# Moving the side jobs of two attention layers to other steps, with the first layer's layer norm on GpSimd

## What is computed

```python
x = _layernorm(x + _L0_attn_ref(x, ...))
x = _layernorm(x + _L0_ffn_ref(x, ...))
x = _layernorm(x + _L1_attn_ref(x, ...))
x = _layernorm(x + _L1_ffn_ref(x, ...))
...
attn = softmax(einsum('bhnd,bhmd->bhnm', q, k) * ATTN_SCALE)
out = einsum('bhnm,bhmd->bhnd', attn, v)
return out.reshape(B, N, C) @ w_proj + b_proj
```

## Time and profile before

| | us |
|---|---|
| median of 3 runs | 1456.69 |
| lowest, highest | 1455.31, 1460.36 |
| the profiled execution | 1455.56 |
| its span in the trace | 1453.8 |
| TensorE busy | 1117.4 (77% of the span) |
| VectorE busy | 1095.9 (75%) |
| ScalarE busy | 841.6 (58%) |
| GpSimd busy | 540.3 (37%) |

### The profile page before, as it was taken

One profiled execution on the slowest core, in us unless ns is written; L12 is line 12 of the kernel. 1 busy time (PEld: TensorE's weight loads), 2 busy tenths in 40 slices (PEclk: granted clock), 3 DMA queues, 4 the chain that ended last, 5 costly groups with the idle time before them and its releaser, 6 DMA issues. The chain is left out here.

```text
span 1453.8 us, 36143 instructions
## 1 busy us (share of the span) xinstructions
PE 1117.4 (77%) x11411; PEld 778.6 (54%) x11411; DVE 1095.9 (75%) x2949; ACT 841.6 (58%) x1840; POOL 540.3 (37%) x568
## 2 busy tenths in 40 slices
PE   2699999999999995139999999999999948103220
PEld 1466666666666653126777777777777724002120
DVE  4589999999999976526677676676776756898996
ACT  1277777777777763616666666666666635103554
POOL 5323233332332203154455444554444142003555
PEclk9899999999999998559999999999999978655555
DMA  1655556556465513044444444444444202000111
GB/s 45 151 124 134 137 120 140 126 128 140 116 138 133 116 29 122 11 120 103 115 114 113 108 115 105 116 115 104 119 103 115 67 16 101 0 0 0 30 36 51
DMA packets 122513, 137.26 MB, mean 94 GB/s; under 512 B 12560, under 2 KB 110160, under 8 KB 113232
## 3 DMA queue, kind: packets, MB, share of 16 engines
q1 hardware_dynamic: 121408, 136.45, 38.8%
q10 hardware_dynamic: 1040, 0.00, 0.0%
HBM read 85.03 MB, written 37.75 MB: 84 GB/s over the span
## 5 line engine op out<-in xcount | busy, mean ns | idle before, releaser
L346 DVE TENSOR_REDUCE attn_negmax<-attn_row_ps 128x2 f32<-128x512 f32 (+1 forms) x1024 | 606.5, 618 | 216.0 <-PE attn_row_ps L527 203.6
L290 ACT ACTIVATE attn_probs<-attn_col_ps 128x512 f32<-128x512 f32 (+1 forms) x1024 | 539.9, 547 | 238.0 <-PE attn_col_ps L549 221.3
L527 PE MATMUL attn_row_ps<-k_st,q_st 72*128 72x256 bf16 (+1 forms) x2048 | 368.0, 261 | 15.3 <-DMA k_st<-attn_scratch 13.9
L549 PE MATMUL attn_col_ps<-q_st,k_st 74*128 74x256 bf16 (+1 forms) x2048 | 368.7, 261 | 2.7 <-ACT attn_probs L290 1.0
L566 PE MATMUL attn_out_ps<-attn_probs,v_sb 128*32 128x256 f32 (+1 forms) x4096 | 247.3, 359 | 1.3 <-ACT attn_probs L290 1.3
L549 PEld LDWEIGHTS attn_col_ps<-q_st,k_st 74*128 74x128 bf16 x2048 | 179.4, 98 | 91.6 <-ACT attn_probs L290 32.3
L527 PEld LDWEIGHTS attn_row_ps<-k_st,q_st 72*128 72x128 bf16 x2048 | 201.1, 99 | 40.7 <-issue 15.3
L275 POOL TENSOR_TENSOR attn_rstd<-attn_var,minus_half 128x2 f32<-128x2 f32 x64 | 45.5, 711 | 384.2 <-DVE attn_var L410 384.2
L523 PE MATMUL attn_row_ps<-mask_qk,ident_h 128*128 128x256 bf16 x512 | 140.8, 275 | 18.4 <-DMA k_st<-attn_scratch 17.8
L566 PEld LDWEIGHTS attn_out_ps<-attn_probs,v_sb 128*32 128x32 f32 x4096 | 106.9, 109 | 86.2 <-issue 20.4
L545 PE MATMUL attn_col_ps<-mask_kq,ident_h 128*128 128x256 bf16 x512 | 141.5, 276 | 13.8 <-DMA q_st<-attn_mT_sb 11.6
(11 more groups left out here) (228 smaller groups left out, 1687.2 us busy)
## 6 DMA issues: line engine op xcount, KB each, us to landing
q_st<-attn_scratch SPq DMA_DIRECT2D x192, 192.0 KB
k_st<-attn_scratch SPq DMA_DIRECT2D x192, 192.0 KB
attn_scratch<-attn_parts SPq DMA_DIRECT2D x64, 384.0 KB, 3.0
attn_scratch<-attn_parts SPq DMA_DIRECT2D x64, 128.0 KB, 3.7
x_in<-in_L_attn_x_dram SPq DMA_DIRECT2D x32, 128.0 KB, 2.1
x_all<-in_L_attn_x_dram SPq DMA_DIRECT2D x32, 128.0 KB, 7.0
moe_xs<-x_all SPq DMA_DIRECT2D x8, 512.0 KB, 3.0
x_in<-x_mid SPq DMA_DIRECT2D x32, 128.0 KB, 2.1
```

The source lines that it names most:

```text
L290: nc.scalar.activation(probs[:, u % 2, j, 0:W], col_ps[:, n % 2, 0:W], ACT.Exp, scale=scale).then_inc(probs_kept, 1)
L346: nc.vector.tensor_reduce(negmax[:, t, 2 * p:2 * p + 2], row_ps[:, row_bank(st, u), 0:2 * keys].rearrange("p (a k) -> p a k", a=2), AX_X, ...
L527: last = nc.tensor.matmul(bank[:, a * keys:(a + 1) * keys], q_st[0:KROWS, sl, h, t * P:(t + 1) * P], k_st[0:KROWS, sl, h, 0:keys], start=n ...
L549: last = nc.tensor.matmul(bank[:, t * N:(t + 1) * N - first], k_st[0:rows, sl, h, t * P:(t + 1) * P], q_st[0:rows, sl, h, first:N], start= ...
```

## The change

The diff below is cut to its core. The table moves side jobs on three engines; the placing L225 is moved ahead of the store L218 and L220 in both layers; the copies of q and k and of the value sums on ScalarE are each cut into two halves with a position of their own; `probs` gets a third buffer; in the second layer the sums of units 0 and 1 stand behind each other at position 7, so that there are three blocks per step and not four; the addition of the epsilon moves from VectorE to GpSimd in both layers; and in the first layer the normalisation is done by GpSimd in two instructions over both token tiles, where VectorE did it in one for each tile.

```diff
@@ the table @@
-AT = {"attn0": dict(act_xT=0, act_mT1=1, act_qk=2, act_oT=3, act_onT=8, act_mT0=11,
...
+AT = {"attn0": dict(act_xT=0, act_mT1=2, act_qk=(2, 3), act_oT=(3, 4), act_onT=9, act_mT0=11,
...
+                    pe_pv={2: [(4, 3)], 7: [(3, 0), (3, 1)], 15: [(3, 2)]})}
+PROBS = 3
+LN_ON_POOL = ("attn0",)
@@ SyncE @@
+                if st.has(2):
+                    sp.wait_ge(mT_kept, st.seq(2, 2, 1))
+                    sl = st.slot(2)
+                    sp.dma_start(q_st[KROWS:KROWS + MROWS, sl, 0:NH, :], mT_sb[:, 0, :]).then_inc(m_placed[0][sl], 16)
                 if st.has(0):
                     sl = st.slot(0)
                     sp.wait_ge(lo_kept, st.seq(0, c=1))
...
-                if st.has(2):
-                    sp.wait_ge(mT_kept, st.seq(2, 2, 1))
-                    sl = st.slot(2)
-                    sp.dma_start(q_st[KROWS:KROWS + MROWS, sl, 0:NH, :], mT_sb[:, 0, :]).then_inc(m_placed[0][sl], 16)
@@ GpSimd @@
+                    pool.wait_ge(mv_kept, st.seq(4, TB, TB))
+                    apart(pool, mem)
+                    nc.gpsimd.tensor_scalar(var[:, :], mv[:, :, 1], EPS, 0.0, ALU.add, ALU.add).then_inc(var_kept, 1)
                     pool.wait_ge(var_kept, st.seq(4, c=1))
                     nc.gpsimd.tensor_tensor(rstd[:, :], var[:, :], mem["minus_half"][:, 0:TB], ALU.pow)\
                         .then_inc(rstd_kept, 1)
+                    if name in LN_ON_POOL:
+                        pool.wait_ge(rstd_kept, st.seq(4, c=1))
+                        nc.gpsimd.tensor_tensor(y_sb[:, :, :], y_sb[:, :, :],
+                                                mv[:, :, 0:1].broadcast_to([P, TB, C]), ALU.subtract)\
+                            .then_inc(centred, 1)
+                        pool.wait_ge(centred, st.seq(4, c=1))
+                        nc.gpsimd.tensor_tensor(x_all[:, bass.ds(st.seq(4, TB), TB), :], y_sb[:, :, :],
+                                                rstd[:, :].unsqueeze(2).broadcast_to([P, TB, C]), ALU.mult)\
+                            .then_inc(ln_kept, TB)
@@ ScalarE @@
-                            wait(act, pv_ready, st.seq(3, 4, u - 1))
+                            wait(act, pv_ready, st.seq(3, 4, u + 1 - PROBS))
...
-                        nc.scalar.copy(oT_sb[:, :], out_ps[:, :]).then_inc(oT_kept, 1)
+                            nc.scalar.copy(oT_sb[:, g * N:(g + 1) * N], out_ps[:, g * N:(g + 1) * N])\
+                                .then_inc(oT_kept, 1)
@@ VectorE @@
+                if name in LN_ON_POOL:
+                    wait(dve, ln_kept, st.seq(4, TB))
...
-                dve.wait_ge(mv_kept, st.seq(4, TB, TB))
-                wait(dve, rstd_kept, st.seq(4))
-                nc.vector.tensor_scalar(var[:, :], mv[:, :, 1], EPS, None, ALU.add).then_inc(var_kept, 1)
...
-                    if n == at["dve_ln"] and st.has(4):
+                    if name not in LN_ON_POOL and n == at["dve_ln"] and st.has(4):
@@ TensorE @@
-                    if n in (at["pe_pv"], at["pe_pv"] + 4, at["pe_pv"] + 8) and st.has(3):
-                        sum_values(st, 3, (n - at["pe_pv"]) // 4)
+                    for lag, u in at["pe_pv"].get(n, ()):
+                        if lag == 3 and st.has(3):
+                            sum_values(st, lag, u)
```

55 lines of the change are left out of this document (31 added, 24 removed).

## The result

| | before | after |
|---|---|---|
| median, us | 1456.0 | 1421.24 |
| lowest, highest, us | 1455.04, 1460.36 | 1421.07, 1426.96 |
| runs | 4 | 4 |
| profiled execution, its span, us | 1455.56, 1453.8 | 1421.07, 1419.3 |

The ratio is 0.9765, with a 95% interval from 0.9734 to 0.9797: 34.8 us or 2.4% faster. The forecast was 1435 with a range of 1418 to 1450.

What follows compares the result with a forecast made beforehand. TensorE's stream plus its waits was taken to bound the step in both layers. From the profiled 1455.56 us, -6 + 1.3 - 12 - 5 - 6 + 7 gave 1435 us, range 1418 to 1450.

Steps and rivals of the forecast that it cites:

- The placing: Second layer, position 0: the placing issued first and maxima split earlier remove the 0.42 us wait; -12 us.
- The first layer: First layer's steps: stream, ScalarE waits and the second transposition's wait sum to -0.2 us a step; -6 us in 30 steps.
- the stream: First layer, TensorE: moving the transposition behind a pair lengthens its stream by 0.2 us a step.
- the waits ahead of column scores: First layer, ScalarE: 0.2 to 0.3 us of waits a step taken as gone, 0.25 in the sum.
- the wait before the second transposition: First layer, second half of the maxima: the wait of 0.35 us becomes 0.2, so -0.15 us a step.
- GpSimd's addition over two numbers: First layer, the epsilon's addition moved to GpSimd: estimated at 0.3 us from a line through two measured sizes.
- The new wait: Second layer, first transposition at position 9: GpSimd's L263 holds cast or subtraction, 0.25 us a step; +7 us.
- Three blocks: Second layer's sums: a joint block saves one entry and one exit, 0.2 us a step; -6 us.
- The fill of the second layer: Second layer's fill: placing no longer behind the store gives 3.6, earlier split about 1.4 more; -5 us (3 to 6).
- The ends: First layer's end: nothing hides GpSimd's normalisation, which takes the place of VectorE's 0.60 us; +1.3 us, once.
- Rival 3: Both layers: waits move to ScalarE, first layer gives nothing and second only half; 1447 us, chance 0.18.

Runs made afterwards that it cites:

- e1: The kernel before with one edit in both layers, the placing issued ahead of the store of the parts; 1438.2 us, ratio 0.9867.
- e2: The changed kernel with the store of the parts issued ahead of the placing again in both layers; 1451.72 us, ratio 0.9967.
- e4: The changed kernel with the first layer's normalisation back on VectorE at position 15; 1420.7 us, ratio 0.9753.
- e9: As e4, with GpSimd's bias for the next residual issued behind its last part of q and k; 1421.71 us, ratio 0.9755.
- e6: The changed kernel with the second layer's first transposition of maxima at position 8 instead of 9; 1441.13 us, ratio 0.9894.
- e10: As e1, with the third buffer of probabilities and the changed kernel's positions of the second layer's value sums; 1436.28 us, ratio 0.9857.
- e3: The changed kernel with the second layer's value sums of units 0 and 1 apart, at positions 7 and 10; 1451.16 us, ratio 0.9955.
- e8: The changed kernel with the first layer's value sums of units 0 and 1 together at position 9, not 8 and 10; 1423.38 us, ratio 0.9773.
- e11: As e6, with VectorE's division in the second layer at position 6 instead of 7; 1425.13 us, ratio 0.9779.
- e5: The changed kernel with the normalisation on GpSimd in the second layer too; 1427.06 us, ratio 0.9788.
- e7: The changed kernel with the second layer's value sums in two joint blocks a step and first transposition at position 8; 1437.66 us, ratio 0.9875.

## Why the prediction was right and wrong

- **The placing** (-12): right, 0.455 us a step by e1. The reason was incomplete. It was read as a wait of one transfer behind two issues; e1 and e2 show a ring through GpSimd and the queue that bounded the whole step. Had the prediction read it as a ring, it would have shown that no other saving counts while the ring stands.
- **The first layer** (-6): the steps of 15.05 came out at 15.06, from 15.23 (the prediction's 15.26 before has no working). By the distances on TensorE the stream got 0.2 us longer, as taken, the waits ahead of column scores about 0.2 shorter for 0.25, and the wait before the second transposition 0.14 shorter for 0.15. What is left of that wait is 0.18 us for the 0.2 taken; cast and subtraction changed parts, and the maxima are ready 3.82 us after the residual's start (301.06 to 304.88) where 3.85 to 4.0 was worked out. GpSimd's addition over two numbers took 0.22 for the estimate of 0.3. The rule of the Trainium skill that spoke against this part (GPSIMD Engine Reference, section 8) says that GpSimd contends with VectorE instructions that have two SBUF inputs. The trace agrees: the subtraction of the second layer is held (1.16 us for 0.17). But e4 shows that VectorE doing the work itself gains nothing while the bias stands there, and e9 that the gain lies in what stands beside the split.
- **The new wait** (+7): the term that failed. Its measured size is 0.03 us a step, +1. Both moments were right, the end of the hold at 10.9 us after position 0 (860.30 less 849.39) and TensorE's arrival at about 10.9 (0.31 behind the row score of 860.00). What was mis-sized is the wait between them. The prediction takes 0.15 us between two dependent instructions, so a hold until 10.9 to 11.1 and an arrival at 10.9 give it at least 0.15; how it came to 0.25 it doesn't say. The rows show 0.05 us from the end of the subtraction to the start of the transposition. This term is 6 of the 14 us. The risk was real: 0.6 us earlier it costs 0.57 (e6).
- **Three blocks** (-6): 0.24 us a step for the 0.2 taken, and 0.21 in the undisturbed steps of e10. What I had not priced is that the joint block is the cover of L522 and L485, 0.59 us a step (e3), and that without the new positions it drives every fourth or fifth subtraction into the next GpSimd instruction (e10).
- **The two projections behind attention**: not foreseen. From L522 to the next scores 0.27 became 0.23, from L528 0.50 became 0.44, 3 us in all. The first depends on what stands ahead: it is 0.27 right behind a block of sums (before, and e8's first layer) or behind a wait (e3), and 0.22 behind a pair without one (after, e10). No experiment isolates the second.
- **The fill of the second layer** (-5): 7.7, and the 4.62 us are gone entirely. The order alone gives 5.8 of it: from ScalarE's first instruction to the 34th mark 66.60 us before, 60.78 in e1, 65.16 in e2, 58.87 after. From the first row score to position 0 the two kernels with the store ahead take 17.2 us (before, e2) and the twelve with the placing ahead 12.7 to 14.6. Ahead of that row score the fourteen kernels scatter from 28.0 to 29.5 us without a pattern. The kernel before has one of the high values (29.46) and the changed kernel the lowest (27.98), so 1.5 of the 7.7 may be chance. The granted clock scatters too: before, it fell to 0.50 at 646 to 648 us, ahead of the stall, and was back at 656 to 658; after, it stayed at 0.50 until 644 to 646 and then at 1.00. The sum had no term for it.
- **The ends**: the normalisation on GpSimd cost 1.0 us once for the 1.3 taken: from the last residual's start to the normalisation's end 2.97 us before (551.02 to 553.99) and 4.00 after (545.47 to 549.47). Of that 0.85 is left at the second layer's first instruction. Rival 3 is refuted by the steps, and all waits of the column scores' matmuls for ScalarE sum to 1.2 us. Their weight loads wait more than before, 57.7 us for 32.3, but that is hidden behind matmuls.

At the first layer's end the two executions also differ in the granted clock, 0.62 and 0.53 in the two stretches from 534 to 538 us before and 1.00 after, so part of the 1.78 us gained there may be the clock's. Of the 1.87 us behind the 61st mark, 2.1 are gained by the 64th, in the last steps of the second layer, and 0.2 are lost behind it. Roughly, the miss of 14 us is the new wait (6), the two projections (3), the fill (3), and the placing and the blocks (2 to 3).

## What to carry to other kernels

When a wait returns once a step, follow its releaser back until the chain closes or leaves the step. If it closes, the ring's length is the step, and no other saving counts until it is cut. And a block of work has two prices: its own time, and the waits of whoever it covers. Price both before moving it, and when moving small VectorE instructions look at what GpSimd runs at that moment, by the hundredth of a microsecond. And look at the steps one by one: two kernels with the same mean step, e1 and e10, were made up of quite different steps.

## What the runs showed of the hardware

**Whether a GpSimd instruction holds a small VectorE one is decided within 0.01 us.** In e6 all 25 subtractions beside L271 start 0.02 to 0.09 us behind its start and take 1.10 to 1.17 us, until 0.03 after its end. In e11 all 25 start 0.02 ahead and take 0.17. In e10 18 start 0.02 ahead and two 0.006 and 0.007 behind, all of 0.17; five start 0.007 to 0.015 behind and take 1.17 to 1.18. Not every GpSimd instruction holds: 30 casts of the changed kernel's second layer start 0.1 us into the power L286 (0.71 us over two numbers) and take 0.17.

**TensorE's clock falls and rises at other moments in each execution.** The first layer's program is the same in the changed kernel, e3, e5 and e6, and the first transposition starts within 0.3 us in all (61.49 to 61.73), but the second at 79.30, 79.11, 85.34 and 79.37. (In e7 and e11, with the same program, they start at 62.75 and 80.36, at 62.64 and 84.54.) Stretches of 2 us (length, busy PE, granted clock, DMA share, GB/s) of the kernel before, then the changed one:

```profile
66.00:68.00 2.00, 2.00 (x20) 0.79 0.77 152
```

```profile
66.00:68.00 2.00, 2.00 (x11) 0.50 0.76 154
...
70.00:72.00 2.00, 2.00 (x19) 0.57 0.74 137
```

and of e5 and e8:

```profile
82.00:84.00 2.00, 2.00 (x11) 0.50 0.00 0
```

```profile
60.00:62.00 2.00, 2.00 (x12) 1.00 0.92 243
```

Ahead of the fill TensorE stands 13.9 us for its first stacked loads, and at 52 to 56 us the granted clock falls to 0.50, that is 1.2 GHz. It is back at 2.4 GHz by 68 us in the kernel before, by 72 in the changed one, by 66 in e4 and only by 92 in e5; in e2 and e8, which stand as long (14.0 and 13.7 us), it didn't fall at all. TensorE was busy without a gap in each of these rows. What decides it no run shows. The mark of the second transposition moves by up to 9 us with it. That accounts for the fill that seemed 1.97 longer, since e1, with the old table, has a late mark too (78.79) and e8, with the new one, an early one (77.27). It may also be why runs of one kernel lie up to 13 us apart (e3); one execution of each was traced, so that isn't shown. Differences of a few microseconds between such kernels are better read from the steps than from the times.
